# One wide row per edge end in place of an aggregate by node and a node stage; the last hop scatters its rows to the output

## The reference, cut to what matters

```python
# layer 0, per edge
ni, nj = x[src], x[dst]
f = elu(concat([ni, nj, ni - nj, edge_attr[:, :65]]) @ Wf + bf) * (edge_attr[:, 0:1] < 8)
a = tanh((ni @ Wq) * (f @ Wk) * 128 ** -0.5 @ Wa)
s = exp(a) / exp(segment_sum(a, src, N))[src]
x = x + (x + segment_sum(s * f, src, N)) @ Wu + bu
x = layernorm(x)
# layer 1, h = x as (N, 4 heads, 32); both directions of every edge, e: (E, 4, 1)
src2, dst2 = concat([src, dst]), concat([dst, src])
e2 = concat([e, e]) / segment_sum(concat([e, e]), dst2, N)[dst2]
e3 = where(src2 == dst2, 0, e2)              # the loops have weight 0
f = lambda y: segment_sum(y[src2] * e3, dst2, N)
k1 = f(h); k2 = f(h + k1 / 3); k3 = f(h + k2 - k1 / 3); k4 = f(h + k1 - k2 + k3)
y = h + (k1 + 3 * (k2 + k3) + k4) / 8
out = layernorm(x + y)
```

## Time and profile before

| | us |
|---|---|
| median of 3 runs (3970.05 to 3972.2) | 3970.56 |
| the profiled execution: from first to last instruction | 3962.0 |
| POOL busy, 2952 instructions | 2931.1 (74%) |
| DVE busy | 2318.4 (59%) |
| ACT busy | 1213.3 (31%) |
| PE busy | 879.3 (22%) |

### The profile page before, as it was taken

The page is one execution under the profiler, slowest core; times in us unless marked ns, Lnnn a source line. Parts: engine busy times, 40 slices in busy tenths (PEclk is TensorE's granted clock), DMA queues, the critical chain, the costliest instruction groups (busy, mean ns, idle before and its releaser), DMA issues.

```text
span 3962.0 us, 26422 instructions
## 1 busy us (share of the span) xinstructions
PE 879.3 (22%) x5636; PEld 748.5 (19%) x5636; DVE 2318.4 (59%) x6450; ACT 1213.3 (31%) x2640; POOL 2931.1 (74%) x2952
## 2 busy tenths in 40 slices
PE   3756787765785000000000000000000000000000
PEld 3755676654554000000000000000000000000000
DVE  6867656655997045555566665666656666533333
ACT  1213777733776001111122221222212222133334
POOL 5677777776777777777677776777767777677776
PEclk8877988888998555555555555555555555555555
DMA  8533433334876013333366665566654444455555
GB/s 270 138 65 64 82 65 69 68 70 118 254 254 190 3 41 106 106 106 106 119 209 211 207 212 178 205 212 211 212 181 149 158 159 159 156 144 158 159 159 139
DMA packets 311971, 581.68 MB, mean 147 GB/s; under 512 B 93856, under 2 KB 172246, under 8 KB 311810
## 3 DMA queue, kind: packets, MB, share of 16 engines
q1 hardware_dynamic: 192034, 394.81, 29.4%
q0 software_dynamic: 116576, 169.55, 18.6%
q10 hardware_dynamic: 3200, 15.63, 1.2%
HBM read 332.00 MB, written 247.75 MB: 146 GB/s over the span
## 4 chain that ended last, share of the span: by engine, by line
POOL 55%; issue 18%; DMA 1%; DVE 1%; ACT 0%; POOLq 0%; PE 0%; DVEq 0%; ACTq 0%
POOL gx L1140 37%; POOL edge_s L898 10%; POOL ag L1357 9%; DVE psum L1245 0%; DMA u<-cross,first_idx 0%; DMA gx<-u,far_row 0%; DVE us L1255 0%; DMA total<-cross_sum,first_idx 0%; DVE psum L1226 0%; DVE tn L1210 0%; DMA u<-us 0%; ACT psum L1191 0%; ACT normed L850 0%; DMA out_dram<-normed 0%; DVE psum L1237 0%
## 5 line engine op out<-in xcount | busy, mean ns | idle before, releaser
L1140 POOL DMA_INDIRECT gx<-u,far_row x1176 | 1109.8, 944 | 368.8 <-issue 357.5
L1226 DVE TENSOR_TENSOR psum<-gx,psum 128x1024 f32<-128x1024 f32 (+1 forms) x200 | 241.6, 1208 | 710.9 <-DMA gx<-u,far_row 505.0
L1191 ACT ACTIVATE psum<-us 128x512 f32<-128x512 f32 x288 | 173.1, 601 | 1186.1 <-DVE tn L1210 626.4
L898 POOL DMA_INDIRECT edge_s<-edge_d,edge_id x392 | 376.4, 960 | 126.0 <-issue 119.2
L1140 POOL DMA_INDIRECT gx<-x,far_i x392 | 373.3, 952 | 119.5 <-issue 119.5
L1357 POOL DMA_INDIRECT ag<-total,fin_idx x390 | 368.9, 946 | 123.1 <-issue 118.5
L1245 DVE TENSOR_TENSOR_SCAN psum<-goes_on,psum 128x1024 f32<-128x1024 f32 (+1 forms) x200 | 449.1, 2245 | 2.2
L1161 PE MATMUL psum<-last_z,chain 128*128 128x128 f32 x8 | 3.2, 501 | 2002.9 <-DVE last_z L1251 2002.9
L1161 PEld LDWEIGHTS psum<-last_z,chain 128*128 128x128 f32 x8 | 2.0, 311 | 2003.9 <-DVE last_z L1251 2003.9
L333 POOL DMA_INDIRECT agg<-summed,sc_idx x196 | 313.3, 1598 | 78.4 <-issue 63.8
L1179 ACT COPY goes_on<-cont_in 128x1024 f32<-128x1024 f32 (+1 forms) x200 | 202.8, 1015 | 387.2 <-DVE cont_in L1024 194.2
(11 more groups left out here) (178 smaller groups left out, 3076.0 us busy)
## 6 DMA issues: line engine op xcount, KB each, us to landing
u<-us SPq DMA_DIRECT2D x144, 512.0 KB, 3.0
total<-tn SPq DMA_DIRECT2D x144, 512.0 KB, 3.1
tp<-total SPq DMA_DIRECT2D x98, 512.0 KB, 5.4
ag<-agg SPq DMA_DIRECT2D x65, 396.0 KB
x<-normed SPq DMA_DIRECT2D x65, 387.0 KB, 3.0
xc<-x SPq DMA_DIRECT2D x65, 387.0 KB, 4.6
tp<-u SPq DMA_DIRECT2D x49, 512.0 KB, 4.6
xc<-in_x_dram SPq DMA_DIRECT2D x65, 384.0 KB
```

Of the source, the lines that this page charges most:

```text
L898: g.indirect_dma_start(edge_s[:, c, :], None, edge_d[:, :], bass.IndirectOffsetOnAxis(ap=edge_id[:, c:c + 1], axis=0)).then_inc(edge_in[k ...
L1140: g.indirect_dma_start(gx[b % 4][:, j * width:(j + 1) * width], None, source[:, :], bass.IndirectOffsetOnAxis(ap=idx[:, c:c + 1], axis=0)) ...
L1226: return v.tensor_tensor(zf.rearrange("p (h f) j -> p j h f", h=H), by_head(gxv(b % 4)[:, c0:c1, 0:D]), per_head(wt[:, b * B + c0:b * B + ...
```

## The change

The indirect DMAs, the sort and the order of rows are reorganized:

- `rows_e` in DRAM has one row of 264 floats (1056 bytes) per edge end, 2e for src and 2e+1 for dst of edge e: the message (zero for dst), its attention, the four edge weights, x of the end's node, and in column 0 or 263 the number of the far end's node row. Stage 1 gathers x[src], x[dst] straight into such rows in SBUF (`pt`, 6 buffers), fills in the rest and stores them with two plain DMAs per step. `same`, the sums over it, `agg`, its scatters, and the histogram are gone.
- Codes of the sort are now node and edge end (16 bits), with the sign for one half of the nodes. A second sort over the same array, by edge end, with each node's last sorted position as payload, gives every end the position of its own node; `far_ends` swaps the two of an edge, and five DMAs write 25000 pairs of 8 bytes into `rows_e`. The first sort begins 3 pieces ahead of step 0, the second at step 21, and its result is stored at step 40.
- Stage 2 is `own_*`: GpSimd gathers the wide rows by sorted edge end (392 DMAs of 128 x 1056 bytes, 5 buffers). Scans add up attention and messages per node; x + decay * sum is made for each of the 50176 sorted positions, multiplied, normalized and stored as `x1s`. A correction of one row per partition follows, by one gather and one scatter.
- The hops gather `x1s` and `u` by sorted position. During hops 0 to 2 a dense pass (`d_*`, 131 chunks of up to 384 rows, one per block) makes layernorm(2 layernorm(x + x Wu + bu)) for all nodes and writes `out`.
- Hop 3 keeps its sum in SBUF, makes the normalized row of every sorted position (`o_*`) and scatters it to `out[node]` (8 plain scatters per block, `o_put`); for positions that aren't a node's last the index is over the bound, and the row is dropped. Stage 4 is gone.

The core of the diff:

```diff
@@ stage 1, gpsimd
-                    for j in range(Q):
-                        g.indirect_dma_start(agg[:, :], bass.IndirectOffsetOnAxis(
-                            ap=sc_idx[:, s * Q + j:s * Q + j + 1], axis=0),
-                            summed[s % NSUM][:, j, :], None, compute_op=ALU.add).then_inc(scat[s % 2], 16)
+                    for r in range(2):
+                        for j in range(Q):
+                            g.indirect_dma_start(pt[i][:, j, r, FX:FX + D], None, x[:, :], bass.IndirectOffsetOnAxis(
+                                ap=idx[:, r, s, j:j + 1], axis=0)).then_inc(x_in[i], 16)
@@ stage 1, sync
+                for s in range(NS):
+                    i = s % NPT
+                    sp.wait_ge(z_set, s + 1)
+                    for r in range(2):
...
+                            sp.dma_start(to, held_rows).then_inc(put_out[i], 16)
@@ stage 1, vector
+                    for n, first in ((0, -AHEAD), (1, SORT2)):
+                        if max(first, 0) <= s < first + SORT_STEPS:
+                            sort_some(n, s - first)
+                    if s == DECODE:
+                        decode()
+                    if s == DECODE + 1:
+                        chains()
+                    if s == DECODE + 2:
+                        end_rows()
+                    if s == SPREAD:
+                        far_ends()
@@ stage 2, gpsimd
-            for c in range(C):
...
-                g.indirect_dma_start(edge_s[:, c, :], None, edge_d[:, :], bass.IndirectOffsetOnAxis(
-                    ap=edge_id[:, c:c + 1], axis=0)).then_inc(edge_in[k % 4], 16)
+            for b in range(NB):
+                if b >= NG:
+                    g.wait_ge(s_res, b - NG + 1)
+                for j in range(B):
+                    c = b * B + j
+                    g.indirect_dma_start(gs[b % NG][:, j, :], None, rows_e[:, :], bass.IndirectOffsetOnAxis(
+                        ap=edge_id[:, c:c + 1], axis=0)).then_inc(x_in[b % NG], 16)
@@ stage 2, vector
+                    v.tensor_tensor_scan(a_run[:, cols], cont[:, cols], gs[b % NG][:, :, FA],
+                                         a_run[:, b * B - 1:b * B] if b else 0.0, ALU.mult, ALU.add).then_inc(s_a, 1)
...
+                    v.tensor_tensor_scan(z, goes_on[b % 2][:, :], z, 0.0, ALU.mult, ALU.add).then_inc(s_run, 1)
...
+                    v.tensor_tensor(da[b % 3][:, :, 0:D], zf.rearrange("p f j -> p j f"),
+                                    da[b % 3][:, :, D].unsqueeze(2).to_broadcast([128, B, D]), ALU.mult
+                                    ).then_inc(s_da, 1)
@@ stage 2, tensor
+                for j in range(B):
+                    o = turned_psum[:, j * 128:(j + 1) * 128]
+                    pe.matmul(o, da[b % 3][:, j, 0:D], ident[:, :], start=True, stop=False)
+                    t = pe.matmul(o, gs[b % NG][:, j, FX:FX + D], ident[:, :], start=False, stop=True)
@@ hops, vector
+                    if h < 3:
+                        d_vector(v, done + b)
+                    if h == 3 and b >= 2:
+                        o_shifts(v, b - 2)
+                    if h == 3 and b >= 1:
+                        o_rows(v, b - 1)
@@ hop 3, gpsimd
+        def o_put(g, k):
+            g.wait_ge(o_normed, k + 1)
+            for j in range(B):
+                c = k * B + j
+                g.indirect_dma_start(out[:, :], bass.IndirectOffsetOnAxis(ap=out_idx[:, c:c + 1], axis=0),
+                                     normed[k % 3][:, j, :], None, bounds_check=N - 1, oob_is_err=False
+                                     ).then_inc(put_rows[k % 3], 16)
...
+                    if h == 3 and b >= 4:
+                        o_put(g, b - 4)
@@ output
-                    for r in range(RR):
-                        at = fin_rest[:, :] if s == NCH else fin_idx[:, s * R + r:s * R + r + 1]
-                        g.indirect_dma_start(ag[s % 4][0:P, r, 0:D], None, total[2][:, :],
-                                             bass.IndirectOffsetOnAxis(ap=at, axis=0)).then_inc(o_row[s % 4], 16)
```

More of the change, by code:

```diff
@@ L17 @@
 EF = 65
+EPS = 1e-5
 Q = 4
@@ L173, in build @@
[L173 to L178 removed]
+        pos_i = sb("pos_i", [128, SN], I32, held)
+        part_i = sb("part_i", [128, 1], I32, held)
+        row_i = sb("row_i", [128, C], I32, held)
+        row_f = sb("row_f", [128, C], F32, held)
@@ L231, in build, with attr_count, put_count @@
-        PREFIX = HIST0 + 1 + HISTN
+        def attr_count(s):
+            return (s // 4 + 1) * 16 + (16 if s == NS - 1 else 0)
+        def put_count(i):
+            return sum(64 if s == NS - 1 else 32 for s in range(i, NS, NPT))
         with nc.Block() as block:
@@ L435, in _ @@
-                    if s == PREFIX:
-                        pe.wait_ge(cnt_set, 1)
-                        pe.matmul(side[0:HI, 0:1], after[0:HI, 0:HI], balance[:, 511:512], start=True, stop=True
-                                  ).then_inc(base_done, 1)
-                        pe.wait_ge(dec_set, 3)
-                        pe.transpose(side[:, 128:256], key0[:, :], ident[:, :]).then_inc(key0_done, 1)
-                add_up(NS - 1)
+                    for n, first in ((0, -AHEAD), (1, SORT2)):
+                        if first + TURN0 <= s < first + SORT_STEPS:
+                            turn(n, s - first - TURN0)
@@ L469, in signs @@
[L469 to L479 removed]
+                act.dma_start(w_raw[:, :, :], Wf[0:3 * D, :].rearrange("(k p) n -> p k n", p=128)).then_inc(w_in, 16)
@@ new lines, in build, with rows_landed, da_stored @@
+        decay1 = sb("decay1", [128, 1], F32, stage)
+        x_a0 = sb("x_a0", [128, D], F32, stage)
+        xa_t1 = sb("xa_t1", [128, 128], F32, stage)
+        tail_junk = sb("tail_junk", [128, H, C], F32, stage)
+        def rows_landed(b):
+            return (len(range(b % NG, NS, NPT)) * Q * 2 + times(b, NG) * B) * 16
+        def da_stored(b):
+            return put_count(b % 3) + times(b, 3) * 16
+        x1_out = [sem(f"s_x1_out{i}") for i in range(3)]
+        (s_on, s_copied, s_first, s_run, s_last, s_a, s_dec, s_far, s_da, s_turned, s_turned_sb, s_mm, s_res,
+         s_stat, s_mv, s_log, s_rstd, s_shift, s_normed) = (
+             sem("s_" + n) for n in ("on", "copied", "first", "run", "last", "a", "dec", "far", "da", "turned",
+                                     "turned_sb", "mm", "res", "stat", "mv", "log", "rstd", "shift", "normed"))
@@ L1160, in hop_tensor @@
+            def hop_tensor(pe):
+                if h < 3:
+                    for b in range(NB):
+                        d_tensor(pe, done + b)
                 pe.wait_ge(last_kept, (h + 1) * NPC)
-                pe.matmul(carry, chain[:, :], last_z[:, :], start=True, stop=True).then_inc(carried, 1)
+                pe.matmul(carry, chain[:, :], last_z[:, 0:D], start=True, stop=True).then_inc(carried, 1)
             def summed_up(i, n):
```

1747 lines of the change are left out of this document (929 added, 818 removed).

## The result

The changed kernel takes 3647.64 us (median of 4 runs, 3646.04 to 3650.76) against 3970.31 for the kernel before in the same session (3964.82 to 3972.2): a ratio of 0.919, 95% interval 0.9176 to 0.9202. It is faster by 322.7 us; the forecast of 3635 was 12.6 us low, and the range of 3545 to 3860 holds the time.

A forecast was written before the change was run, and what follows sets the result against it. GpSimd's pitch between indirect DMAs bounds the kernel: 532 us edge stage, 502 own rows, 44 to hop 0, 1534 for hops 0 to 2, 490 + 514 + 10 for hop 3 and the end, 8.6 around the span: 3635 us, range 3545 to 3860.

The forecast's parts named there:

- The count of DMAs alone: Whole kernel: 196 accumulating scatters at 1.86 us leave GpSimd, a gain of 365 us.
- the edge stage: First stage: GpSimd's 392 gathers at 1.27 us, 498 us, set its length; the second stage starts at 532 us.
- the term around the span: Outside the profiled span: 8.6 us between span and median time, left as they are.
- the one for the pairs: Edge stage, step 40: the 8-byte pairs take between nothing and 100 us of queue time, none on the path.
- the two-port rule of the prediction: Gathers beside VectorE: its two-port mode shuts GpSimd out of writing descriptors, 26 ns a gather, about 35 us in the sum.
- Own rows: Second stage: 392 gathers of 1056-byte rows at 1.28 us, 502 us, no price for width, other engines under GpSimd's pace.
- rival B: An engine holds a stage: own rows 676 us with TensorE at 1.2 GHz, or edge stage + 40 to 80; 14%.
- The bubble: Between the last wide gather and hop 0: 44 us for blocks in flight and the corrected first row.
- The scatter's pitch: Hop 3: a plain scatter costs near a gather, 1.31 us, so 392 scatters take 514 us.
- A: Hop 3: the plain scatter costs like the accumulating one, + 216 us, total 3850 us; 14%.
- C: Hop 3: rows dropped by the bounds check are free, 136 us less than at 1.25, total 3475 us; 7%.
- D: Hop 3: scatters can't be pipelined, each waits 3.0 us for its landing, + 1176 us, total 4811 us; 4%.

The follow-up runs named there:

- f1: Changed kernel with the 8-byte pairs written in eight slices, one behind the row stores of each of steps 40 to 47; run alone: 3627.76 us, ratio 0.914.
- e3: Changed kernel without the second sort, burst of pairs kept, so the far rows are wrong ones: 4500.24 us, ratio 0.974 to the kernel before.
- f3: The changed kernel without the second sort, as in e3, run again in another group: 4443.16 us, ratio 0.964 to the kernel before.
- e4: Changed kernel with four kinds of scatter in hop 3: as it is 1024 ns, no check 975, check dropping none 1249, with addition 1611.
- e1: Changed kernel without the pair DMAs, rows stored whole, every far row being row 0: 5154.91 us, ratio 1.116 to the kernel before.
- e6: Changed kernel without the pair DMAs, far rows being each node's own last row, so spread: 4460.99 us, ratio 0.967 to the kernel before.
- the groups: Experiments run together, all slowed by a condition of open cause: the kernel before took 4606 to 4620 us, the unedited changed kernel 4489.76, ratio 0.972.

## Why the prediction was right, and where it was off

**The bound and the count.** Right: 2760 instructions on GpSimd, one pitch, and next to nothing of other engines in the chain of waits (POOL 59%, issue 21%, DVE and DMA 1% each). The count of DMAs alone gave 365 us, and 323 came. That the total is only 12.6 us off is partly luck: the edge stage was 40.9 us late and hop 3 6.9, and 34.8 us of it were cancelled by four smaller misses the other way, 9.8 of them the term around the span, which took a short execution for one like the median's.

**The edge stage.** This is the step that failed, by 40.9 us, and the term is the one for the pairs: "between nothing and 100 us of queue time, I take none on the path, since only tile 47 needs a store that stands behind them, 60 us later". The queue time was 48.4 us, in the middle of the bounds. The argument for none on the path fails by the prediction's own numbers: 60 us are the whole lead of the 6 buffers, but the same paragraph puts VectorE 25 to 35 us behind GpSimd at step 40, so only 25 to 35 us were left. Measured: when step 40's stores go out at 465.4, GpSimd is already at tile 44; the burst begins at 467.7, tile 47 was due at 494.3, 26.6 us later, and 48.4 us of burst end at 516.1. The runs split the 40.9: 19.5 went with the slices of f1. The rest, 21.4, is by f1's rows: 514.67 - 5.41 = 509.3 us for the gathers in place of 498 (1.30 instead of 1.27 each), and 38.8 in place of 28 for the tail and the change of block, since slices still stand before the last stores. Without the second sort the stall before tile 47 stayed (39 us in e3 and f3), but only under the condition; how much of the lead VectorE's lag took in the first run is not shown.

**VectorE and the sorts.** That VectorE would not stop GpSimd was right: but for tile 47 the edge gathers waited only 1.2 us for row stores in the first run. What the second sort costs seems to come by slower gathers: the edge gathers have a mean of 992 ns between 231 and 440 us, beside the second sort, and 944 between 460 and 494. In own rows VectorE is nearly as busy (366 of 490 us, against 168 of 209 beside the sort), and the gathers take 947. With e3 and f3 (12 to 16 ns less a gather without the second sort) this points to the kind of VectorE's work and not to how busy it is. Here the forecast took 26 ns from the earlier trace rows for all busy stages, too little for the sort (48) and too much for own rows (3), which is most of the -11.5 us there.

The Trainium skill, "SBUF — State Buffer", "Who interferes with whom", also says that a VectorE instruction with two SBUF inputs contends with a GpSimd one that reads SBUF. The 992 against 944 ns would fit that: the sort's `min` and `max` read two SBUF arrays, the large sums of own rows have one operand in PSUM. The same section infers that such an instruction leaves the writing of descriptors alone, which speaks against it. No run here changes the operands alone, so neither this rule nor the two-port rule of the prediction is shown to be the cause.

**Own rows.** No price for rows of 1056 bytes: right, 947 ns. TensorE kept 0.91 of its clock: rival B's 1.2 GHz did not come. ScalarE was dearer than forecast in one line, the spreading copy of 1024 (L830, which reads the gathered rows with 264 floats from one element to the next and writes PSUM, 2031 ns in place of 1.05 us), and has 357 us of 490 in place of the forecast's 7.3 x 49 = 358, since others were cheaper.

**The bubble, the hops.** 39.8 for 44, and 508.2 us a hop for 511. The 5 us a hop for slower gathers did not come (947 ns beside the dense pass). VectorE still waits 814 us in the hops before L1392, so its dense work is hidden, as was said.

**Hop 3.** The scatter's pitch was 1.01 + 0.30 = 1.31, the value taken. That a plain scatter is near a gather is what e4 shows; the forecast had no price for the bounds check (274 ns there), and the kind that drops rows was 225 ns cheaper than the one that drops none, so 1.31 was right by two terms that the sum did not have. The 6.9 us over are at the end: the forecast had 10 us for all that is not pitch, and 16.9 came, 9.1 of them behind GpSimd's last scatter.

**The rivals.** A (3850) fell with the scatter's 1010 ns, and e4 shows why: the addition is what is dear. C (3475) fell with the same number; a saving by dropped rows, if it is one, is taken up by the check. D (4811) fell: the scatters are pipelined, with 119.8 us of idle time for 392, all issue. B did not come in own rows (clock 0.91, 490.5 us); in the edge stage the 40.9 us are of the size of its + 40 to 80, but 31.8 of them are the wait before tile 47, which went with the slices.

## What to carry to other kernels

Where one queue issues everything, count its instructions first, and price each by kind: a gather, a plain scatter and rows twice as wide were one price here, a bounds check a quarter more, an addition some 60% more. Then look at the queues that only carry: a burst of tiny writes can hold the queue that issues it (25,000 pairs of 8 bytes, 48 us) and whatever stands behind it, so ask for each one which buffer is released by the next store in that queue, and how many tiles ahead the reader already is. Taking out the dearest instructions alone may give back less than their own time where the next engine stands close behind, as the old edge stage suggests.

## What the hardware showed that I had not expected

- A bounds check on an indirect DMA costs GpSimd 274 ns per 128 rows, and a scatter that drops 37% of its rows by it costs 225 ns less than one that drops none (e4; the table written is another one too).
- 25,000 writes of 8 bytes, 0.2 MB, held a hardware queue's issuing for 48.4 us in a burst, with a DMA share of 1.32 between 460 and 520 us. In slices between other stores they took 40. An issue's time does not follow its own pairs: 8192 pairs took 0.80 us as the first of the burst, and 256 pairs 13.20 us near its end, but 0.58 us behind a slice (f1).
- With the hops' gathers reading one and the same row of a table by all 128 partitions, the software queue's packets took 3.6 times as long as with spread rows (2576 us of queue time against 722, e1 and e6, in sum with the gathers that did not change).
- 128 rows of 1056 bytes in one gather cost GpSimd 947 ns, as 128 rows of 512 bytes do.
- In the groups the kernel before took 16% and the changed one 23% longer, with waits without a named end, and with GpSimd's busy time and the queues' time unchanged in the changed kernel (2655.5 and 2653.1 us; 1266 and 1270). A tight comparison needs its control in the same group.
